# The edge attributes of a graph convolution multiplied straight from SBUF, instead of from a PSUM copy

## The reference, cut to what matters

```python
def _nnconv(x, src, dst, edge_attr, ew, eb, rw, rb):      # three times
    W = (edge_attr @ ew + eb).reshape(edge_attr.shape[0], x.shape[1], rw.shape[1])
    xj = x[src]
    msg = jnp.einsum('ei,eio->eo', xj, W)
    agg = jax.ops.segment_sum(msg, dst, num_segments=x.shape[0])
    return agg + x @ rw + rb
...
msg = inputs[src] * timestamp                              # once, the "max" stage
h = jax.ops.segment_max(msg, dst, num_segments=inputs.shape[0])
```

## Time and profile before

| what | value |
|---|---|
| median of three runs | 10953.86 us (10949.11 to 10955.05) |
| the profiled execution, its span | 10954.1 us |
| the three conv loops on GpSimd, first gather issued to last one's end | 168.6 to 2684.9, 3012.0 to 5527.5, 5726.8 to 8243.6 us |
| the max loop, the same | 8425.6 to 10804.2 us |
| busy over the span: PE, DVE, ACT, POOL | 9673.8, 6582.2, 7059.5, 8026.2 us |
| mean granted TensorE clock | 0.962 |

### The profile page before, as it was taken

One profiled execution on the slowest core, in us unless ns is written; L12 is line 12 of the kernel. 1 busy time (PEld: TensorE's weight loads), 2 busy tenths in 40 slices (PEclk: granted clock), 3 DMA queues, 4 the chain that ended last, 5 costly groups with the idle time before them and its releaser, 6 DMA issues.

```text
span 10954.1 us, 169268 instructions
## 1 busy us (share of the span) xinstructions
PE 9673.8 (88%) x49910; PEld 8173.9 (75%) x49910; DVE 6582.2 (60%) x10016; ACT 7059.5 (64%) x7283; POOL 8026.2 (73%) x8404
## 2 busy tenths in 40 slices
PE   5999999997199999999949999999993999999994
PEld 4888888886188888888838888888883888888883
DVE  6767676766266767677737676767673444444442
ACT  3676767675167677777726767676762677777762
POOL 6777777777577777777757777777775777777776
PEclk8999999998599999999979999999996999999997
DMA  4333333333133333333323333333331222222221
GB/s 112 110 106 111 111 110 106 111 111 93 43 106 111 109 107 111 111 107 109 110 64 111 105 112 110 110 106 111 111 104 35 55 55 55 59 58 55 55 55 26
DMA packets 430013, 1000.58 MB, mean 91 GB/s; under 512 B 168672, under 2 KB 268225, under 8 KB 397976
## 3 DMA queue, kind: packets, MB, share of 16 engines
q0 software_dynamic: 268800, 464.14, 18.3%
q1 hardware_dynamic: 161176, 536.02, 14.4%
HBM read 869.94 MB, written 129.62 MB: 91 GB/s over the span
## 4 chain that ended last, share of the span: by engine, by line
POOL 52%; issue 27%; DVE 10%; DMA 8%; PE 1%; DVEq 1%; SPq 0%; POOLq 0%; ACT 0%; ACTq 0%
POOL gathered L517 51%; DVE msg L903 7%; DMA gathered<-conv_table,idx 7%; DVE xe L821 1%; PE pY L434 1%; DVE idx L944 1%; DVEq L211 1%; SPq L231 0%; POOL gathered L1047 0%; PE pY L688 0%; DVE gathered L246 0%; DVE tmp L246 0%; DMA gathered<-in_dst,idx 0%; DMA gathered<-scanned,idx 0%; DMA conv_table<-gathered 0%
## 5 line engine op out<-in xcount | busy, mean ns | idle before, releaser
L688 PE MATMUL pY<-part,hot_key 128*128 128x400 f32 x40672 | 8624.4, 362 | 476.5 <-DVE xe L821 447.9
L688 PEld LDWEIGHTS pY<-part,hot_key 128*128 128x128 f32 x40672 | 7324.8, 189 | 757.2 <-DVE xe L821 593.0
L517 POOL DMA_INDIRECT gathered<-conv_table,idx x5952 | 5641.4, 948 | 2030.8 <-issue 1811.5
L821 DVE TENSOR_REDUCE xe<-pY 128x16 f32<-128x400 f32 x5084 | 2835.2, 567 | 1354.1 <-PE pY L690 1337.0
L568 ACT ACTIVATE apart<-key_pair,zone_lane 128x1408 f16<-128x1408 f16 x1984 | 2804.4, 1461 | 664.6 <-PE pY L690 639.5
L573 ACT ACTIVATE hot_key<-apart 128x1408 fp32r<-128x1408 f16 x1984 | 2612.0, 1365 | 0.0
L517 POOL DMA_INDIRECT gathered<-max_table,idx x1860 | 1812.2, 974 | 610.4 <-issue 566.5
L246 DVE TENSOR_TENSOR gathered<-gathered,pT 128x2048 f32<-128x2048 f32 x372 | 851.2, 2288 | 1512.8 <-DMA gathered<-conv_table,idx 1512.8
L690 PE MATMUL pY<-near_mask,not_near 128*128 128x400 bf16 x5084 | 1744.7, 343 | 0.0
L903 DVE TENSOR_REDUCE msg<-gathered 128x256 f32<-128x2304 f32 x744 | 1559.1, 2096 | 0.2
L690 PEld LDWEIGHTS pY<-near_mask,not_near 128*128 128x128 bf16 x5084 | 488.3, 96 | 898.8 <-issue 898.8
(11 more groups left out here) (122 smaller groups left out, 1812.6 us busy)
## 6 DMA issues: line engine op xcount, KB each, us to landing
key_pair<-key_rows SPq DMA_DIRECT2D x248, 1408.0 KB
scanned<-run_pair SPq DMA_DIRECT2D x248, 416.0 KB, 2.5
gathered<-conv_table,idx POOLq DMA_INDIRECT x5952
attr_pair<-in_attr SPq DMA_DIRECT2D x186, 208.0 KB
gathered<-max_table,idx POOLq DMA_INDIRECT x1860
conv_table<-gathered SPq DMA_DIRECT2D x24, 504.0 KB, 3.4
conv_table<-rows SPq DMA_DIRECT2D x18, 504.0 KB, 3.2
gathered<-scanned,idx POOLq DMA_INDIRECT x392, 2.3
```

The source lines that it names most:

```text
L517: e.indirect_dma_start(out=G[s][:, t, 0:width], out_offset=None, in_=table[:, :], in_offset=bass.IndirectOffsetOnAxis(ap=idx[s][:, t:t + 1 ...
L688: e.matmul(pG[bank], hot_key[s][:, z, at:at + P], part[:, z * NEAR:(z + 1) * NEAR, :], start=(z == 0 and k == 0), stop=False)
L821: e.tensor_reduce(xe[s][:, j * D:(j + 1) * D], pG[j % BANKS].rearrange("p (r d) -> p d r", d=D), AX.X, ALU.max).then_inc(s_pick.sem, 1)
```

## The change

In the conv loops the copy L774 is taken out of ScalarE's program, with the wait ahead of it. VectorE's multiply takes its second operand from `attr[s]`, a view of `attr_pair` in SBUF, instead of `pA` in PSUM. Its first wait is now for the attribute load itself (`loaded`) in place of `s_factors`. The multiply signals a new semaphore, `s_attr_read`, in place of the counted mark `m_g`, and the wait that follows it is on that semaphore, so `MARKS` is 3 in both kinds of loop. SP may now load the attributes of the next pair only when ScalarE's `pe_attr` copy and VectorE's multiply of the pair's second chunk are both done. The max loop stays as it was. The core of the diff:

```diff
             def sp_body(e, i, more_keys, more_attr):
                 if more_attr:
-                    gate(e, "sp", s_factors, i * SLOTS + (b_fac + SLOTS))
+                    if is_max:
+                        gate(e, "sp", s_factors, i * SLOTS + (b_fac + SLOTS))
+                    else:
+                        gate(e, "sp", s_pe_factors, i * SLOTS + (b_pefac + SLOTS))
+                        gate(e, "sp", s_attr_read, i * SLOTS + (b_read + SLOTS))
                     load_attr(e, i + 1)
...
                     e.copy(pe_attr[s][:, :, 0:EF], attr[s][:, tg:T, :]).then_inc(s_pe_factors.sem, 1)
-                    gate(e, "act", s_multiplied, number(c) * 2 + b_mul)
-                    e.copy(pA[:, 0:tg * EF], attr[s][:, 0:tg, :].rearrange("p t f -> p (t f)")
-                           ).then_inc(s_factors.sem, 1)
...
-            MARKS = 3 if is_max else 4
+            MARKS = 3
...
-                gate(e, "dve", s_factors, n + (b_fac + 1))
+                if is_max:
+                    gate(e, "dve", s_factors, n + (b_fac + 1))
+                else:
+                    gate(e, "dve", loaded, i * 16 + 16)
                 gate(e, "dve", got[s], i * (16 * tg) + 16 * tg)
...
-                    factors = pA[:, 0:tg * EF].rearrange("p (t f) -> p t f", f=EF)
+                    factors = attr[s][:, 0:tg, :]
...
-                    m_g = mark(tt(e, g4[:, 0:tg, :, 0:EF], g4[:, 0:tg, :, 0:EF],
-                                  factors.unsqueeze(2).to_broadcast([P, tg, D, EF]), ALU.mult))
+                    tt(e, g4[:, 0:tg, :, 0:EF], g4[:, 0:tg, :, 0:EF],
+                       factors.unsqueeze(2).to_broadcast([P, tg, D, EF]), ALU.mult).then_inc(s_attr_read.sem, 1)
                     next_picks(2)
-                    need(m_g)
+                    gate(e, "dve", s_attr_read, n + (b_read + 1))
                     m_tg = total(0, tg)
```

More of the change, by code:

```diff
@@ L192, in build @@
         s_factors = sem("s_factors")
+        s_attr_read = sem("s_attr_read")
         s_pe_factors = sem("s_pe_factors")
@@ L624, in edges @@
                 c.n for c in (s_gath, s_pick, s_xt, s_xeT, s_prod, s_abs))
-            b_fac, b_pefac, b_mul = s_factors.n, s_pe_factors.n, s_multiplied.n
+            b_fac, b_pefac, b_mul, b_read = s_factors.n, s_pe_factors.n, s_multiplied.n, s_attr_read.n
             loaded = sem(f"s_attr_{name}")
@@ L975, in edges @@
             bump(s_abs, CHUNKS * ZONES * 2)
-            bump(s_factors, CHUNKS)
+            bump(s_factors if is_max else s_attr_read, CHUNKS)
             bump(s_multiplied, CHUNKS if is_max else 2 * CHUNKS)
```

## The result

The changed kernel takes 11284.42 us at the median of four runs (11283.08 to 11285.11) beside 10954.28 for the kernel before: ratio 1.0301, 95% interval 1.0289 to 1.0314. The forecast was 11284 us. The profiled execution's span is 11281.3 us against 10954.1, 327.2 more. The experiments ran in five groups, each beside runs of the kernel before of its own, and that kernel took 10959 us in the second group but 16189 to 16878 us in the other four, so a run is compared only within its group; ratios leave out runs over 1.5% above the fastest of their kernel, which medians and ranges include.

A forecast was written before the change was run, and what follows sets the result against it. GpSimd's gathers were taken to bound the kernel. Held gathers add 333 and 21 us, 354 in all, less 24 us given back from the scans: 10954 + 330 = 11284 us, +3.0%, range 11,230 to 11,390.

The forecast's parts named there:

- The bound: Conv loops: GpSimd's gathers and gaps, 20.2 of a chunk's 20.3 us, set the pace; GpSimd is never held up.
- The removed copy is worth nothing: ScalarE's L774, 372 times, some 100 us busy, is off the path: cost and gain nothing.
- The multiply's length: VectorE's multiply with both operands in SBUF takes 2.29 us, as against 2.289 with one in PSUM.
- The waits: The attribute load moves behind the pair's second multiply, lands with 3 us to spare before its first reader; cost nothing.
- The collision: Gathers starting during the two-SBUF-operand multiply end 0.82 us after it: 318 delayed 1.05 us, 51 delayed 0.42, sum 354 us.
- the forecast's own bounds: Variations on the sum: 26 or 21 us less, 37 to 74 more for a later scan, 11 more for ten won races.
- The scans: Conv loops: in the new rhythm a gather just escapes the scan, giving back the 24 us that scans cost before.
- It takes no lock: Rival, 6%: the multiply's broadcast, stride-nine operands leave the gathers alone at 0.94 us; time stays 10954 us.
- VectorE wins the race: Rival, 3%: the multiply starts before the second gather has read its indices and holds it too; 11,730 us if always.
- The scan collided once: Rival, 6%, that the scan collides too: coming 0.8 us later it costs 288 us more, 11,570 us.
- TensorE did not bind: Rival, 2%, that TensorE or the clock becomes the bound: near 39 us a chunk at half the clock.

## Why the prediction was right, point by point

- **The bound.** Right. In the changed kernel GpSimd's waits for the indices are still 0.3 us at most, and the growth of its gathers is the growth of the span (328.0 against 327.2 us).
- **The removed copy is worth nothing.** Right in the time: nothing of the 327.2 us is left for it to have given. ScalarE's busy time fell by 79.0 us (7059.5 to 6980.5), not 100: the 372 copies lasted 100.4 us in all, but the records of ScalarE's neighbouring instructions overlap with them.
- **The multiply's length.** 2.293 us against 2.289 before and the 2.29 assumed.
- **The waits.** Right. The load goes out 0.27 us after the multiply (1018.33 against 1015.77 + 2.29) and lands in 2.5 us, the value borrowed from the larger store. Nobody waits for it; its first reader, the copy, starts at 1024.02. The key load follows at 1019.74.
- **The collision.** Right in place, sign and size: 318 + 51 gathers as forecast, each ending 0.82 us after the multiply. Their delays come to 332 and 22 us where the forecast had 333 and 21. The net sum was 330; the page gives 330.7. That the total agrees within 1 us is luck, for the forecast's own bounds were 11 to 74 us each; that the terms agree one by one is not.
- **The scans.** Right, and by as little as was said: the gather behind the scan starts 0.82 us into it, and of the 369 that start inside a scan one is lengthened, by 0.11 us. That a margin of 0.01 us held was luck as much as reckoning.
- **The rivals.** "It takes no lock" fell with the 2.05 us gather, for a broadcast operand takes it as well as a plain one. "VectorE wins the race" did not occur: in four chunks the second gather started 0.004 to 0.014 us after the multiply and still went first, inside the 0.04 us that the forecast allowed. Second gathers are long only at the long gap. The scan collided once. TensorE did not bind in the runs the forecast was made for; it and waits without a visible cause do in the other condition, where the ranges of the two operands overlap. The forecast said nothing of such a condition, and it holds only where GpSimd binds.

All of this was reasoned from rows of the kernel before. What the experiments add is that the length of one instruction sets the price: the same work in two instructions costs 89 us instead of 330. And with the operand alone exchanged, gathers are held or not.

## What to carry to other kernels

Before moving an operand of a VectorE instruction from PSUM to SBUF, look at what GpSimd does meanwhile: with both operands in SBUF the indirect DMA that it starts next waits for that instruction's end, and the length of the single instruction is the price. Where GpSimd's issuing sets the pace, as here, a ScalarE copy that nobody waits for is cheaper than the held gathers. If the SBUF form is wanted, cutting the instruction so that the next gather starts before the second piece does recovers most (241 of 330 us here). Work out phases with their spread, and take borders from records: a mean of 1.12 us beside a border at 1.17 that was taken to be at 1.23 hid a fifth of the chunks.

## What the runs showed of the hardware that was not expected

Of two back-to-back halves the second starts 1.14 us after the first, though the first's record is 1.225 us long. A gather that starts up to 1.16 us in goes before it and delays it by up to 0.07 us; one from 1.18 us on is held until the second half's end and 0.82 us more. The same kernel took 10,959 us in one group and 16,189 to 16,878 us in the others, where VectorE and ScalarE wait with nothing in the profile that releases them (4.41, 9.55 and 16.45 us in the lines above). In that condition less work on TensorE did not bring GpSimd back as the bound.
